# A decoder layer with routed experts on one core: keys of tile 1 padded first, weight splitting dealt out through the routing, picked rows added two tiles at a time

## What is computed

```python
x = x + attn(layernorm(x))            # 16 query heads, 4 key groups, rope, window 64 with 4 sink tokens
x = x + cross(layernorm(x), ctx, ctx) # 16 heads of 16, causal
x = x + ffn(layernorm(x))             # shared expert (704) times a sigmoid, plus top 4 of 16 experts (176 each)

def ffn(h):
    shared = (silu(h @ g.T) * (h @ u.T)) @ d.T * sigmoid(h @ sgate.T)
    w, ids = top_k(softmax(h @ gate.T), 4)
    for e in range(16):
        coef = sum(where(ids == e, w, 0))
        sparse += coef * ((silu(h @ w13[e][:176].T) * (h @ w13[e][176:].T)) @ w2[e].T)
    return shared + sparse
```

## Time and profile before

| | |
|---|---|
| median of 3 runs | 352.58 us (351.36 to 354.53) |
| the profiled execution | 351.55 us |
| its span, first to last instruction | 349.7 us |
| mean granted PE clock | 0.957 of full speed |
| PE busy | 310.2 us (89%), 2596 matmuls |
| DVE busy | 243.7 us (70%), 733 instructions |
| ACT busy | 186.6 us (53%), 537 instructions |
| POOL busy | 148.6 us (42%), 179 instructions |
| moved by DMA | 66.84 MB, mean 191 GB/s |

### The profile page before, as it was taken

The page is one execution under the profiler, slowest core; times in us unless marked ns, Lnnn a source line. Parts: engine busy times, 40 slices in busy tenths (PEclk is TensorE's granted clock), DMA queues, the critical chain, the costliest instruction groups (busy, mean ns, idle before and its releaser), DMA issues.

```text
span 349.7 us, 8490 instructions
## 1 busy us (share of the span) xinstructions
PE 310.2 (89%) x2596; PEld 240.8 (69%) x2596; DVE 243.7 (70%) x733; ACT 186.6 (53%) x537; POOL 148.6 (42%) x179
## 2 busy tenths in 40 slices
PE   7858799999999997869998869999999999999953
PEld 3334577667676864648785668888978899898732
DVE  2352878888888979662887956676766776663785
ACT  1034589898988968463587434444434444432110
POOL 3580424445355404487377653433434434433000
PEclk9986999999999999995999989999999999999996
DMA  7996078989797951023022426767777777763921
GB/s 209 316 392 264 2 222 222 276 222 318 229 294 244 247 172 32 16 94 112 32 96 102 146 66 183 233 226 233 211 228 215 222 231 228 231 216 103 396 106 60
DMA packets 44185, 66.84 MB, mean 191 GB/s; under 512 B 5379, under 2 KB 32020, under 8 KB 43636
## 3 DMA queue, kind: packets, MB, share of 16 engines
q1 hardware_dynamic: 39508, 54.91, 52.1%
q0 software_dynamic: 3792, 10.56, 8.0%
q10 hardware_dynamic: 848, 0.92, 1.2%
HBM read 37.07 MB, written 29.30 MB: 190 GB/s over the span
## 4 chain that ended last, share of the span: by engine, by line
PE 31%; issue 25%; POOL 19%; DVE 14%; ACT 5%; DMA 4%; SPq 0%; POOLq 0%; DVEq 0%; ACTq 0%
POOL y_picks L609 13%; POOL x_slots L534 5%; PE bank L1422 5%; PE bank L1496 5%; PE bank L1413 4%; PE bank L1366 4%; ACT probs L646 3%; PE bank L1431 2%; PE bank L1455 2%; DVE neg_max L897 2%; PE bank L1534 2%; PE bank L1470 2%; PE bank L1408 1%; DVE yg L1308 1%; DMA yg<-y_picks 1%
## 5 line engine op out<-in xcount | busy, mean ns | idle before, releaser
L609 POOL DMA_INDIRECT y_picks<-yb,ids x47 | 45.1, 960 | 67.5 <-DVE yb L1275 66.8
L646 ACT ACTIVATE probs<-bank,neg_max 128x128 f32<-128x128 f32 x256 | 70.6, 398 | 3.0 <-DVE neg_max L897 2.8
L897 DVE TENSOR_REDUCE neg_max<-bank 128x4 f32<-128x512 f32 x64 | 42.2, 683 | 11.0 <-PE bank L1413 10.9
L1769 PE MATMUL bank<-w,hbt 128*128 128x256 f32 x188 | 48.2, 380 | 0.0
L1422 PE MATMUL bank<-ident,probs 128*128 128x128 f32 x256 | 38.5, 289 | 3.7 <-ACT probs L646 3.7
L534 POOL DMA_INDIRECT x_slots<-x,slots x32 | 36.6, 1142 | 9.3 <-issue 8.6
L1422 PEld LDWEIGHTS bank<-ident,probs 128*128 128x128 f32 x256 | 30.3, 147 | 12.1 <-ACT probs L646 10.0
L806 ACT ACTIVATE xbt_h<-bank 128x256 fp32r<-128x256 f32 x47 | 18.0, 384 | 35.8 <-PE bank L1739 35.7
L1769 PEld LDWEIGHTS bank<-w,hbt 128*128 128x128 f32 x188 | 32.1, 190 | 2.5
L1268 DVE TENSOR_TENSOR hb<-sg,bank 128x176 f32<-128x176 f32 x47 | 15.9, 338 | 23.3 <-ACT sg L814 23.3
L814 ACT ACTIVATE sg<-bank 128x176 f32<-128x176 f32 x47 | 14.9, 317 | 29.4 <-PE bank L1496 29.4
(11 more groups left out here) (175 smaller groups left out, 691.1 us busy)
## 6 DMA issues: line engine op xcount, KB each, us to landing
x_slots<-zero_b SPq DMA_DIRECT2D x16, 1072.0 KB, 10.6
w<-w_in_dram SPq DMA_DIRECT2D x47, 256.0 KB, 3.0
xb<-x_slots SPq DMA_DIRECT2D x47, 134.0 KB
w<-w_in_dram SPq DMA_DIRECT2D x4, 1408.0 KB, 12.4
yg<-y_picks SPq DMA_DIRECT2D x8, 512.0 KB, 6.7
sw_raw<-shared_in_dram SPq DMA_DIRECT2D x6, 384.0 KB, 3.4
ktc<-keys_in_dram SPq DMA_DIRECT2D x8, 256.0 KB, 2.9
ctx_sb<-ctx_in_dram SPq DMA_DIRECT2D x1, 1024.0 KB, 12.8
```

Source lines behind the costliest of these rows:

```text
L609: pool.indirect_dma_start(y_picks[:, :], bass.IndirectOffsetOnAxis(ids[:, n:n + 1], 0), yb[:, n % RB, :], None).then_inc(yb_placed[n % RB] ...
L646: ins = act.activation(probs[:, g, j, :], ps_s[kind][g][:, 128 * j:128 * j + 128], ACT.Exp, bias=neg_max[:, kind, g, j:j + 1])
L897: dve.tensor_reduce(neg_max[:, kind, g, :], ps_s[kind][g].rearrange("p (j n) -> p j n", j=BLK), AX.X, ALU.max, negate=True).then_inc(max_r ...
L1769: ins = pe.matmul(ps_yb[n % 2][:, 0:D], hbt[:, n % 2, k, :], w2[:, n % RB, k, :], start=k == 0, stop=k == KC - 1)
```

## The change

Six edits. The first is in iteration 0, the next two are in the routing, the rest are in the end.

- DVE pads tile 1's keys before iteration 0. In iteration 0 `first_norms` of tiles 4 to 7 goes behind the last row maximum. PE gets 7 and 5 matmuls of zeros at two places of iteration 0, and `front_a(2)` waits for the normalised tile 2 explicitly.
- On PE the up part of the shared expert's chunk 0 goes behind the scores of the last cross tile.
- ACT's `high_experts` and DVE's `low_expert` are dealt out in other portions.
- The picked rows are added for two tiles with one instruction, so 12 instructions stand in place of 24, and they are interleaved with the shared expert's second half one by one.
- The second half's copy of bank 1 goes from DVE to ACT.
- The first four tiles are stored with two transfers.

```diff
-WARM = (13, 3, 22, 3)
+WARM = (13, 3, 22, 3, 7, 5)
...
@@ SP @@
+            for pair in range(HB // 2):
+                sp.wait_ge(x_out_ready, pair + 1)
+                sp.dma_start(out[2 * pair:2 * pair + 2].rearrange("b p d -> p b d"), x2[:, 2 * pair:2 * pair + 2, :]
+                             ).then_inc(y_stored, 16)
+            for b in range(HB, B):
...
@@ ACT @@
                 act.wait_ge(down_done, (half + 1) * SC)
-                act.activation(y_t[:, 0, :], ps_y[0][:, :], ACT.Copy).then_inc(yt_ready, 1)
+                for m in range(1 + half):
+                    act.activation(y_t[:, m, :], ps_y[m][:, :], ACT.Copy).then_inc(yt_ready, 1)
...
-            high_experts(2, 4)
+            high_experts(2, 5)
             high_hidden(2)
             gate(3)
+            high_experts(5, 7)
             high_hidden(3)
-            high_experts(4, 6)
             gate(4)
+            high_experts(7, 9)
             high_hidden(4)
-            high_experts(6, 10)
+            high_experts(9, 12)
             gate(5)
             high_hidden(5)
-            high_experts(10, NE)
+            high_experts(12, NE)
...
@@ DVE, iteration @@
                 if isinstance(t, int) and t == 0:
-                    first_norms(LATER[1])
                     dve.wait_ge(rstd1_ready, 2)
...
-                if on(t, t + 1):
+                if on(t, t + 1) and not (isinstance(t, int) and t == 0):
                     front_p(t + 1)
...
                     row_max(SELF, t, 3)
+                if isinstance(t, int) and t == 0:
+                    first_norms(LATER[1])
...
             front_p(0)
+            front_p(1)
             iteration(0)
...
@@ DVE, routing @@
             low_hidden(2)
+            low_expert(3)
             gated(3)
+            low_expert(4)
             low_hidden(3)
             route_slots(2)
-            low_expert(3)
+            low_expert(5)
             gated(4)
+            low_expert(6)
             low_hidden(4)
-            low_expert(4)
             block_counts()
-            low_expert(5)
+            low_expert(7)
             gated(5)
...
-            for e in range(6, 10):
-                low_expert(e)
+            low_expert(8)
             gated(SC)
-            finish(0)
+            low_expert(9)
+            finish()
+            low_expert(10)
             low_hidden(SC)
-            low_expert(10)
...
@@ DVE, end: pick_halves, pick_sums, add_picks are combine's three steps over bs = two tiles @@
+                for b in (2 * pair, 2 * pair + 1):
+                    dve.wait_ge(gathered[b], 16)
+                link(dve.tensor_tensor(yg[:, bs, 0:2, :], yg[:, bs, 0:2, :], yg[:, bs, 2:4, :], ALU.add))
...
@@ PE @@
                 if isinstance(f, int) and f == 2:
+                    pe.wait_ge(xn1_ready, 3)
...
                     front_c(t + 1)
+                if isinstance(t, int) and t == 0:
+                    keep_clock(WARM[4], ps_s[CROSS][3])
...
                     third_norm(t - 3)
+                if isinstance(t, int) and t == 0:
+                    keep_clock(WARM[5], ps_s[CROSS][3])
...
-            rows_of(0)
+            rows_of(0, (0,))
...
             third_norm(B - 3)
+            rows_of(0, (1,))
             transpose_probs(CROSS, B - 1, 0)
```

More of the change, by code:

```diff
@@ L452, in _ @@
                              ).then_inc(gathered[b], 16)
-            for b in range(B):
-                sp.wait_ge(x_out_ready, b + 1)
+            for pair in range(HB // 2):
[3 more added lines that the diff above has]
+            for b in range(HB, B):
+                sp.wait_ge(x_out_ready, HB // 2 + b - HB + 1)
                 sp.dma_start(out[b], x2[:, b, :]).then_inc(y_stored, 16)
-            sp.wait_ge(y_stored, 16 * B)
+            sp.wait_ge(y_stored, 16 * (HB // 2 + HB))
         @block.gpsimd
@@ L1172, in low_hidden, with finish @@
                                   ).then_inc(hidl_ready, 1)
-            def finish(half):
-                dve.wait_ge(down_done, (half + 1) * SC)
+            def finish():
+                dve.wait_ge(down_done, SC)
                 dve.tensor_copy(y_t[:, 1, :], ps_y[1][:, :]).then_inc(yt_ready, 1)
@@ L1301, in _ @@
             take_block(NBLK - 1)
-            def combine(first, last):
-                for b, step in (divmod(i, 3) for i in range(first, last)):
-                    if step == 0:
-                        dve.wait_ge(gathered[b], 16)
-                        link(dve.tensor_tensor(yg[:, b, 0:2, :], yg[:, b, 0:2, :], yg[:, b, 2:4, :], ALU.add))
-                    elif step == 1:
-                        link(dve.tensor_tensor(yg[:, b, 0, :], yg[:, b, 0, :], yg[:, b, 1, :], ALU.add))
-                    else:
-                        ins = dve.tensor_tensor(x2[:, b, :], yg[:, b, 0, :], x2[:, b, :], ALU.add)
-                        if b < HB:
-                            ins.then_inc(x_out_ready, 1)
-                        else:
-                            link(ins)
@@ L1318, in _, with pick_halves @@
-            dve.wait_ge(rows_added, HB)
-            done = 0
-            for n, more in zip(range(SC + AHEAD, 2 * SC), (6, 6, 6, 0)):
-                gated(n)
-                low_hidden(n)
-                combine(done, done + more)
-                done += more
-            combine(done, done + 3)
-            finish(1)
-            combine(done + 3, 3 * B)
+            def pick_halves(pair):
+                bs = slice(2 * pair, 2 * pair + 2)
+                for b in (2 * pair, 2 * pair + 1):
+                    dve.wait_ge(gathered[b], 16)
+                link(dve.tensor_tensor(yg[:, bs, 0:2, :], yg[:, bs, 0:2, :], yg[:, bs, 2:4, :], ALU.add))
@@ new lines, in pick_sums, with add_picks @@
+            def pick_sums(pair):
+                bs = slice(2 * pair, 2 * pair + 2)
+                link(dve.tensor_tensor(yg[:, bs, 0, :], yg[:, bs, 0, :], yg[:, bs, 1, :], ALU.add))
+            def add_picks(pair):
+                bs = slice(2 * pair, 2 * pair + 2)
+                ins = dve.tensor_tensor(x2[:, bs, :], yg[:, bs, 0, :], x2[:, bs, :], ALU.add)
+                if pair < HB // 2:
+                    ins.then_inc(x_out_ready, 1)
+                else:
+                    link(ins)
@@ new lines, in _ @@
+            dve.wait_ge(rows_added, HB)
+            gated(SC + 2)
+            low_hidden(SC + 2)
+            pick_halves(0)
+            gated(SC + 3)
+            pick_sums(0)
+            low_hidden(SC + 3)
+            add_picks(0)
+            gated(SC + 4)
+            pick_halves(1)
+            low_hidden(SC + 4)
+            pick_sums(1)
+            add_picks(1)
+            gated(SC + 5)
+            pick_halves(2)
+            low_hidden(SC + 5)
+            pick_sums(2)
+            add_picks(2)
@@ L1328, in _ @@
+            pick_halves(3)
+            pick_sums(3)
+            add_picks(3)
             for pair in range(2):
@@ L1528, in ranks, with keep_clock @@
                 ins.then_inc(rank_psum, 1)
-            def keep_clock(n):
+            def keep_clock(n, bank=ps_s[SELF][0]):
                 for _ in range(n):
-                    pe.matmul(ps_s[SELF][0], zero_b[:, 0:128], zero_b[:, 0:HALF], start=True, stop=True)
+                    pe.matmul(bank, zero_b[:, 0:128], zero_b[:, 0:HALF], start=True, stop=True)
             def iteration(t):
```

## The result

The changed kernel takes **341.75 us** (median of 4 runs, 341.07 to 343.41), beside 351.97 for the kernel before (4 runs, 350.68 to 354.53): ratio 0.971 [0.964, 0.978]. The forecast was 341.0. The profiled execution of the changed kernel is the longest of its four, 343.41 with a span of 341.6, against 351.55 and 349.7 before.

What follows compares the result with a forecast made beforehand. No engine bounds the whole: PE bounds iterations and expert blocks, other engines the front and end. 351.55 less 4.0 (iteration 0), 2.5 (routing) and 4.3 (end) is 340.75, given as 341.0; range 336.5 to 346.0.

Steps and rivals of the forecast that it cites:

- Iteration 0, 4.0: Front: new order (2.5 us) and a full clock start tile 0's values at 29.5, not 33.49; bounds 2.5 to 4.5.
- The front's gain is carried through: Iterations and expert blocks are PE's and unedited, so a gain in front of them passes through unchanged.
- Routing, 2.5: Routing: moving chunk 0's up part and dealing out w_l and roundings saves 2.5 us; bounds 0.5 to 4.0.
- The variance's 2.9: Routing: the last tile's variance, at 169.32, comes 2.9 us earlier if the clock holds, 1.4 without.
- Filled, it may keep the clock: Routing: six matmuls filling PE's wait for exponentials may keep the clock, turning 9.10 us at 0.51 into about 4.6.
- The start ... shrinks to 1.8 at the counts: Routing: an earlier start of 2.9 to 3.5 us shrinks to 1.8 at the block counts, as DVE limits.
- is off the path: Routing: with w_l dealt out, POOL's scatters end some 5 us earlier and POOL no longer sets the time.
- The pause before the counts: Routing: PE finishes chunk 5 some 3 us before the counts; a clock drop there takes up to 1.5 us back.
- The end, 4.3: End: paired, interleaved additions and bank 1's copy on ACT save 4.3 us; bounds 2.0 to 5.5.
- bounds 2.0 (the additions alone): End: lower bound, the merged additions by themselves save 2.0 us on DVE.
- The slower rival: Expert blocks: another rhythm, 0.5 us waits for rows in 30 blocks, costs 15 us, giving 355.8; chance 0.04.
- A sign of being wrong: Expert blocks: the prediction is wrong if their 112 us change by more than 2.

Runs made afterwards that it cites:

- experiment 2: The kernel before with one routing edit each: dealing of w_l and roundings alone, ratio 1.003 (+1.0 us); moved up part of chunk 0 alone, 0.993 (-2.5 us).
- the run of four w_l: The changed kernel with four remainders w_l again in one run ahead of the product of chunk 6: 342.67 us in one run.
- logits mixed: The changed kernel with six 512-column matmuls of chunk 1's gate part dealt out between the narrow gate logits of tiles 4 to 6: 0.975 to the kernel before.
- experiment 1: The kernel before with one stage's edits each: front 0.988 (-4.4 us), routing 0.986 (-4.9 us), end 0.985 (-5.3 us).
- the grouped one: The changed kernel with each pair's three additions kept together behind each chunk's remainder, not interleaved one by one: 0.984 to the kernel before.

## Why the prediction was right

- **Iteration 0, 4.0: right, and for its reasons.** Without zeros the values start at 30.7, forecast 31.0 for the order alone. The zeros give 1.8, forecast 1.5. Measured alone, -4.4. The 33.49 that the sum starts from is one execution: five with the old front start between 31.9 and 34.1, 32.8 in the mean, and against that the order gives 2.1 and the whole 3.9. The padding and the move of the statistics weren't run apart.
- **The front's gain is carried through: right.** Alone it reaches the end of the program. In the profiled execution 0.7 of it is missing at the first scatter, by the half-clock stretch at 134.
- **Routing, 2.5: near in size, wrong in two reasons.** In the profile the time from the first scatter to the first block's gate and up matmuls is 57.6 and not 60.1 (198.49 less 140.89, 204.85 less 144.71); in runs, up moved gives -2.5 alone and the dealing +1.0. The variance's 2.9 came as 2.1 on top of the front's 3.8 in the first profile, where POOL still waits 0.88 for it, and as 2.9 in the second (161.84, the first scatter there at 140.16). "Filled, it may keep the clock" failed: with the move the clock falls behind the gate logits in every execution. "The start ... shrinks to 1.8 at the counts" holds: PE's matmuls behind the counts start 5.5 earlier, which is 1.7 on top of the front's 3.8. Before, then now:

```profile
187.55 0.20 PE L1596 MATMUL bank<-counts,upto 16*16 16x1 f32 x2 [1.50 <-DVE counts L1133]
```

```profile
182.06 0.20 PE L1628 MATMUL bank<-counts,upto 16*16 16x1 f32 x2 [1.89 <-DVE counts L1141]
```

  POOL "is off the path" failed as well. The shorter scatter was costed at nothing and the blocks' rows gained 0.5 by it (experiment 2), but POOL's last landing is what SP waits for before it loads them. The working doesn't agree with itself there either: the same paragraph puts 1 us of the sum on that scatter.
- **The pause before the counts.** PE waits 1.89 there in the changed kernel, not 3. In ten executions with the dealing the wait is 1.86 to 1.89; in three of them the clock fell behind it. Without zeros:

```profile
184.06 0.20 PE L1624 MATMUL bank<-counts,upto 16*16 16x1 f32 x2 [1.88 <-DVE counts L1141]
...
185.50:192.50 7.00, 6.80 (x19) 4.97 (x18) 3.16 (x12) 3.37 (x6) 5.47 (x6) 0.51 0.39 116
```

  Those three have 43.5 to 44.6 in the routing's second part, the other seven 40.9 to 42.4. One of the three is the run of four w_l, whose rows came late as well. The other two, one of them with its logits mixed, lie 2.4 and 2.9 above the mean of the seven (41.7), so the forecast's "up to 1.5" for such a fall was low, and it comes at times.
- **The end, 4.3: right total, wrong bound.** The products stand 5.8, 8.4 and 12.5 behind the first, forecast 5.7, 8.5 and 12.5, and the last six matmuls run at a full clock as forecast. What failed is "bounds 2.0 (the additions alone)": merged without the interleaving, the additions gave 0.1 (28.4 to 28.3).
- **Sum.** Front -4.4, up part -2.5, dealing +1.0 and end -5.3 make -11.2; the changed kernel has -10.2 here and -11.3 in its second measurement. With the routing's -4.9 from experiment 1 in place of its two parts the sum is -14.6, so the agreement rests on the choice of the better measured parts. That the stages add up because PE's own stages lie between them is argued, not shown.
- **The slower rival** fell: the blocks' column spans 106.9 to 110.3, which is 0.07 us a block and far from 0.23. Its mechanism exists at that size: PE's waits for rows before transposing are 6.5 us in all in the changed profile, 5.5 before, and without the wait for the first rows 3.9 and 2.1.
- **A sign of being wrong came up.** The prediction calls itself wrong if the blocks' 112 us change by more than 2. In the first profile they do, to 115.15 or 2.45 a block, and with the same code they don't in the second, 112.2 (308.56 less 196.32). The sign was set tighter than one execution differs from the next. That the forecast's 341.0 was met to 0.75 us is partly luck, since two measurements of the same kernel lie 0.9 apart (341.75 and 342.64) and its single runs 5.8.

## What to carry to other kernels

Where the last chain goes from engine to engine and back, look at what stands between its links before making that work shorter: here the merged additions gave 0.1 kept together and 4.7 interleaved. Before an engine is called off the path, look for who waits for its last transfer to land: POOL's shorter scatter moved the blocks' rows little, but they waited for it all the same. The gains of three stages with PE's own stages between them added up here to within 1 us. Cut every profile at the same events before comparing two of them, and take the kernel before more than once too: one execution of this kernel differs from the next by more than some of its edits.

## What the runs showed of the hardware

PE's clock falls to 1.2 GHz at places that the program doesn't fix. Of the fourteen executions five have no such fall in the iterations and take 111.2 there; the others have one or two and take 111.9 to 114.8. Two executions whose code is the same up to the end, the changed kernel's second and the grouped one:

```profile
28.90:140.20 111.30, 101.97 (x1377) 72.58 (x1376) 94.02 (x260) 92.42 (x298) 43.60 (x62) 1.00 0.71 205
```

```profile
28.90:143.70 114.80, 106.46 (x1376) 75.96 (x1376) 94.20 (x260) 92.43 (x298) 43.57 (x61) 0.96 0.70 199
117.75:124.75 7.00, 7.00 (x49) 4.96 (x48) 2.69 (x8) 2.90 (x11) 0.00 (x0) 0.51 0.75 214
138.25:141.75 3.50, 3.38 (x16) 2.85 (x16) 2.82 (x8) 2.15 (x8) 0.00 (x0) 0.52 0.00 0
```

Each of the two stretches follows work that ran at 1.00 in the other execution. Some of the spread of single runs (338.4 to 344.1) is likely to come from there.
